# Cross-attention and a mixture-of-experts FFN on one core: softmax reciprocals spread through DRAM

## What is computed

```
xn    = layernorm(x)
q     = rmsnorm(xn Wq)           # 16 heads of 32
k, v  = rmsnorm(ctx Wk), ctx Wv  # per kind (text, image)
att   = softmax(q k_text / sqrt(32)) v_text + softmax(q k_img / sqrt(32)) v_img
x1    = x + att Wo
x2    = layernorm(x1)
out   = x1 + shared(x2) + sum over a token's 4 experts of weight * expert(x2)
```

## Time and profile before

| | |
|---|---|
| profiled execution, first to last instruction (span) | 1212.8 us |
| its own time | listed with the runs: 1212.84, 1211.41, 1212.59 us; the page gives the span only |
| TensorE, weight loads beside it | 1150.7 us busy (95%), 415.6 (34%) |
| VectorE | 824.9 us busy (68%) |
| ACT | 649.5 us busy (54%) |
| GpSimd | 190.7 us busy (16%) |
| granted TensorE clock, mean | 0.994 |
| DMA | 143.02 MB, mean 118 GB/s |

### The profile page before, as it was taken

The page is one execution under the profiler, slowest core; times in us unless marked ns, Lnnn a source line. Parts: engine busy times, 40 slices in busy tenths (PEclk is TensorE's granted clock), DMA queues, the critical chain, the costliest instruction groups (busy, mean ns, idle before and its releaser), DMA issues. The chain is left out here.

```text
span 1212.8 us, 20795 instructions
## 1 busy us (share of the span) xinstructions
PE 1150.7 (95%) x8484; PEld 415.6 (34%) x8484; DVE 824.9 (68%) x1042; ACT 649.5 (54%) x916; POOL 190.7 (16%) x299
## 2 busy tenths in 40 slices
PE   6899999999999999999999999998999998999996
PEld 2342222444222244422224442222454433333332
DVE  6776878877677887768788777997778852222221
ACT  5558997444899744499864459885121121222221
POOL 1220000143000014300001430001110012333342
PEclk9999999999999999999999999999899999999998
DMA  9851000559200045910004693013823317999742
GB/s 312 178 113 36 2 2 10 131 119 211 36 2 2 11 129 135 205 26 2 2 26 114 147 195 111 2 36 106 329 75 121 115 59 289 357 317 317 243 62 33
DMA packets 140056, 143.02 MB, mean 118 GB/s; under 512 B 107952, under 2 KB 108208, under 8 KB 134960
## 3 DMA queue, kind: packets, MB, share of 16 engines
q1 hardware_dynamic: 134832, 130.78, 36.9%
q0 software_dynamic: 5120, 10.82, 4.7%
HBM read 95.67 MB, written 20.73 MB: 96 GB/s over the span
## 5 line engine op out<-in xcount | busy, mean ns | idle before, releaser
L665 ACT ACTIVATE work<-ps 128x1024 f32<-128x1024 f32 (+1 forms) x416 | 403.0, 1021 | 42.5 <-PE ps L1152 38.8
L1158 PE MATMUL ps<-work,vals 128*32 128x512 f32 (+2 forms) x1664 | 221.0, 603 | 1.2 <-ACT work L665 0.6
L994 PE MATMUL ps<-wts,work 128*128 128x512 f16 x864 | 193.1, 379 | 2.7 <-DVE work L721 2.4
L1152 PE MATMUL ps<-quer,keys 32*128 32x512 f16 x2496 | 171.9, 378 | 16.0 <-ACT work L665 2.8
L900 DVE TENSOR_TENSOR work<-work 128x2048 f32<-128x2048 f32 x64 | 146.6, 2291 | 6.3 <-DVE work L897 0.5
L900 DVE TENSOR_TENSOR attn<-attn,work 128x2048 f32<-128x2048 f32 x62 | 142.0, 2290 | 5.2
L994 PEld LDWEIGHTS ps<-wts,work 128*128 128x128 f16 x864 | 83.8, 98 | 109.7 <-issue 8.3
L1961 PE MATMUL ps<-wring,xgt 128*80 128x512 f32 x256 | 114.9, 592 | 0.0
L586 ACT CAST work<-work 128x512 f16<-128x512 f32 x68 | 42.0, 618 | 130.8 <-DVE work L753 130.8
L994 PE MATMUL ps<-wts,hl 128*128 128x512 f16 x432 | 100.2, 383 | 11.6 <-DVE wts L703 7.5
L1152 PEld LDWEIGHTS ps<-quer,keys 32*128 32x128 f16 x2496 | 46.2, 92 | 185.1 <-ACT work L665 159.9
(11 more groups left out here) (216 smaller groups left out, 1364.7 us busy)
## 6 DMA issues: line engine op xcount, KB each, us to landing
wring<-in_wx SPq DMA_DIRECT2D x32, 1536.0 KB, 8.9
raw<-in_ctx SPq DMA_DIRECT2D x52, 256.0 KB, 3.1
work<-in_x SPq DMA_DIRECT2D x4, 1024.0 KB, 5.3
table<-nums SPq DMA_DIRECT2D x16, 256.0 KB, 2.5
work<-in_x SPq DMA_DIRECT2D x12, 256.0 KB, 5.1
x<-work SPq DMA_DIRECT2D x12, 256.0 KB, 2.6
x2t_rows<-nums SPq DMA_DIRECT2D x12, 256.0 KB, 2.5
x2t<-x2t_rows SPq DMA_DIRECT2D x3, 1024.0 KB, 9.2
```

Source lines behind the costliest of these rows:

```text
L665: act.activation(prob[0:rows, s % PROBS, 2 * half:2 * half + 2, :], ps[0:rows, 2 * pair:2 * pair + 2, :], ACT.Exp, scale=SCALE).then_inc(a ...
L994: mm = pe.matmul(out, lhs(a, c)[:, cols], wts[:, w, z, c * D:(c + 1) * D], start=(k == 0), stop=(k == len(steps) - 1))
L1152: mm = pe.matmul(ps[:, 2 * pair + h % 2, :], k[h * HD:(h + 1) * HD, :], q[h * HD:(h + 1) * HD, :], start=(e == 0), stop=(e == len(terms) - 1))
L1158: return pe.matmul(ps[h * HD:(h + 1) * HD, NUM, :], vals[a:z, ORDER[n], g * P + h * HD:g * P + (h + 1) * HD], prob[a:z, s % PROBS, h, :], ...
```

## The change

- `spread` on TensorE, the 0/1 tiles `sel`, and their banks go. SP stores `rcp` to a DRAM tensor (`store_sums`, in slot 1 of the next batch) and reads it back with the row repeated over 32 partitions: one DMA for each of the four heads h, for two head groups at a time, into a tile `rb`, in slots 1 and 5 (`spread_pair`). The second waits until the first two groups are weighed.
- `weigh(g)` multiplies by `rb` and runs two slots later (slots 3 to 6), with `out_high` and `out_low` behind it; `O_SLOT`, `NORM_SLOT` and `LOW_SLOT` move by two slots as well.
- For the last batch all eight DMAs (two sets of four) are issued ahead of the branch, into a tile `rbl` for all groups.
- Ahead of the branch TensorE computes gate half 0, up half 0 and gate half 1 (`gate`). Behind it `gate_up(1)`, without its gate half, `gate_up(2)` and `gate_up(3)` come before the output products. ACT and VectorE have the shared tiles' work reordered to match; the check matmul comes after the gates.
- Waits for earlier table and row stores move from ACT's to VectorE's list. Expert 2's load moves behind the last normalising. Some semaphores are merged for the second pass.

The core of the diff:

```diff
-O_SLOT = [6, 7, 10, 11]
+O_SLOT = [8, 9, 12, 13]
-NORM_SLOT = [8, 9, 12, 13]
-LOW_SLOT = [9, 10, 13, 14]
+NORM_SLOT = [10, 11, 14, 15]
+LOW_SLOT = [11, 12, 15, 16]
+WEIGH = 3
...
-        self.sel = at("sel", 172 * KB_, [P, NG, 2, P], F32)
+        self.rb = at("rb", 172 * KB_, [P, 2, 2, L], F32)
+        self.rbl = at("rbl", 164 * KB_, [P, NG, 2, L], F32)
...
+            def store_sums(bb):
+                sp.wait_ge(a_rcp, bb + 1)
+                sp.dma_start(r_dram[bb], rcp[:, :]).then_inc(s_rd, 16)
+
+            def spread(dst, bb, pair, landed):
+                for h in range(4):
+                    rows = r_dram[bb][h * HD + 4 * pair:h * HD + 4 * pair + 4, :]
+                    sp.dma_start(dst[h * HD:(h + 1) * HD].rearrange("p g t q -> p (g t) q"),
+                                 rows.unsqueeze(0).to_broadcast([HD, 4, L])).then_inc(landed, 16)
+
+            def spread_pair(bb, q, pair):
+                if pair == 0:
+                    sp.wait_ge(s_zero, 32)
+                    sp.wait_ge(s_rd, 16 * bb)
+                    upto(sp, a_at, q * NG)
+                else:
+                    sp.wait_ge(a_at, gn(q, 1))
+                spread(rb[:, :, :, :], bb - 1, pair, s_rb)
+
+            def last_spreads(bb):
+                store_sums(bb)
+                sp.wait_ge(s_rd, 16 * (bb + 1))
+                for pair in range(2):
+                    spread(rbl[:, 2 * pair:2 * pair + 2, :, :], bb, pair, s_rl[pair])
...
+                        if i == 1 and b > 0:
+                            store_sums(bb - 1)
                         if i >= 1:
                             turn_key(bb, i - 1)
+                        if i in (1, 5) and b > 0:
+                            spread_pair(bb, q, i // 4)
...
                 last_loads(p, bb)
+                last_spreads(bb)
...
             def weigh(q, g):
-                dve.wait_ge(a_sel, gn(q, g))
-                image = own(dve.tensor_tensor(nums[:, g, 1, :], nums[:, g, 1, :], ps[:, NUM, :], ALU.mult))
-                dve.tensor_tensor(nums[:, g, 0, :], nums[:, g, 0, :], ps[:, DEN, :], ALU.mult).then_inc(a_mt, 1)
+                dve.wait_ge(s_rb, 64 * (2 * q + g // 2 + 1))
+                image = own(dve.tensor_tensor(nums[:, g, 1, :], nums[:, g, 1, :], rb[:, g % 2, 1, :], ALU.mult))
+                dve.tensor_tensor(nums[:, g, 0, :], nums[:, g, 0, :], rb[:, g % 2, 0, :], ALU.mult).then_inc(a_mt, 1)
...
-                    if b > 0 and 1 <= i < 1 + NG:
-                        weigh(q, i - 1)
-                    if b > 0 and 2 <= i < 2 + NG:
-                        out_low(q, i - 2)
+                    if b > 0 and WEIGH <= i < WEIGH + NG:
+                        weigh(q, i - WEIGH)
+                    if b > 0 and WEIGH + 1 <= i < WEIGH + 1 + NG:
+                        out_low(q, i - WEIGH - 1)
...
-                    if b > 0 and 1 <= i < 1 + NG:
-                        spread(bb - 1, q, i - 1)
...
-                    steps = [(c, a, z) for c in range(NC) for a, z in PARTS]
-                    for k, (c, a, z) in enumerate(steps):
-                        pe.matmul(ps[:, GATE_BANK, :], swt[SG][:, a, c * D:c * D + P], m.x2t[0][:, :, z, c, :],
-                                  start=(k == 0), stop=(k == len(steps) - 1))
-                    pe.wait_ge(a_rcp, bb + 1)
-                    for t, bank in ((1, SEL_BANK[0][0]), (0, SEL_BANK[0][1])):
-                        pe.matmul(ps[:, bank, :], sel[:, 0, t, :], rcp[:, :], start=True, stop=True)
+                    gate(SG, 0, 0)
+                    pe.wait_ge(f_wlo, 3 * p + 2)
+                    gate(SU, 0, 2).then_inc(s_gate, 1)
+                    gate(SG, 1, 1)
...
+            gate(0)
             weigh(0)
+            gate_low(0)
             weigh(1)
+            gate(1)
             out_low(0)
             weigh(2)
             out_low(1)
+            gate_low(1)
             weigh(3)
             out_low(2)
...
             out_low(3)
-            gate(0)
-            gate_low(0)
-            gate(1)
+            gate(2)
+            gate_low(2)
             out_rows(0)
-            gate_low(1)
             out_norm(0)
             out_rows(1)
             norm_low(0)
             out_norm(1)
+            gate(3)
             out_rows(2)
...
-            for g in range(1, NG):
-                spread(g)
-            gate_up(0)
-            pe.wait_ge(t_mt, 2)
             gate_up(1)
+            gate_up(2)
+            gate_up(3)
             for j in range(QT):
                 output(j)
...
-            gate_up(2)
             turn_out(QT - 1)
             for j in range(3 * QT, NT):
                 rt_last = route(j)
             rt_last.then_inc(e_r, 1)
-            gate_up(3)
             gate_up(4)
```

More of the change, by code:

```diff
@@ L156, in __init__, with attention_program @@
         self.yf = [at(f"yf{i}", o * KB_, [CAP, D], F32) for i, o in enumerate((108, 110, 60, 62))]
-def attention_program(nc, m, d, x1_dram, x2_dram, table, out, s_turned, s_xr):
+def attention_program(nc, m, d, x1_dram, x2_dram, r_dram, table, out, s_turned, s_xr, s_rl, s_gate):
     with ExitStack() as ctx:
@@ L298, in value_bank, with turned, rowed @@
             return NUM if k == KT - 1 else 2 + k % 2
+        def turned(bb):
+            return (bb - B + 1) * (HEADS * QT + 1)
+        def rowed(bb):
+            return (bb - B + 1) * (2 + NG)
         def rows_of(n):
@@ L479, in _ @@
                 sp.wait_ge(s_turned[1], 64)
+                for pair in range(2):
+                    sp.wait_ge(s_rl[pair], 128)
             sp.end_ifs()
@@ L879, in sums_and_results @@
                         ffn_weight(p, g - 1)
+                    if b > 0 and g < 2:
+                        for j in range(2):
+                            dve.wait_ge((s_tab, s_x2)[g][j], 16 * ((out_batch(bb - 1) + 1) * QT // 2))
                     dve.wait_ge(a_img, gn(bb, g))
@@ L929, in maxima @@
                             bank = 4 * (k % 2)
-                            dve.wait_ge(m_sc, n0 + k + 1)
+                            dve.wait_ge(m_sc, turned(bb - 1) + k + 1)
                             flat = ps[:, bank:bank + 4, :].rearrange("p a n -> p (a n)")
@@ L982, in _ @@
                 one_pass(1)
+                for pair in range(2):
+                    dve.wait_ge(s_rl[pair], 128)
             dve.end_ifs()
@@ L1251, in attention, with gate @@
                     pe.wait_ge(f_wlo, 3 * p + 1)
-                    steps = [(c, a, z) for c in range(NC) for a, z in PARTS]
-                    for k, (c, a, z) in enumerate(steps):
-                        pe.matmul(ps[:, GATE_BANK, :], swt[SG][:, a, c * D:c * D + P], m.x2t[0][:, :, z, c, :],
-                                  start=(k == 0), stop=(k == len(steps) - 1))
-                    pe.wait_ge(a_rcp, bb + 1)
-                    for t, bank in ((1, SEL_BANK[0][0]), (0, SEL_BANK[0][1])):
-                        pe.matmul(ps[:, bank, :], sel[:, 0, t, :], rcp[:, :], start=True, stop=True)
+                    gate(SG, 0, 0)
+                    pe.wait_ge(f_wlo, 3 * p + 2)
+                    gate(SU, 0, 2).then_inc(s_gate, 1)
+                    gate(SG, 1, 1)
+            def gate(w, it, bank):
+                steps = [(c, a, z) for c in range(NC) for a, z in PARTS]
+                for k, (c, a, z) in enumerate(steps):
+                    mm = pe.matmul(ps[:, bank, :], swt[w][:, a, c * D + it * P:c * D + (it + 1) * P],
+                                   m.x2t[0][:, :, z, c, :], start=(k == 0), stop=(k == len(steps) - 1))
+                return mm
             def one_pass(p):
@@ L1300, in lay_attention, with ffn_program @@
     }
-def ffn_program(nc, m, d, x1_dram, table, out, s_turned):
+def ffn_program(nc, m, d, x1_dram, table, out, s_turned, s_rl, s_gate):
     with ExitStack() as ctx:
@@ L1491, in norm_store @@
                          ps[:, TURN_BANK[j], :].bitcast(F16)).then_inc(n_out, 1)
-            for g in range(NG):
-                out_high(g)
             gate_tanh(0)
             gate_high(0)
+            out_high(0)
             gate_tanh(1)
+            out_high(1)
             gate_high(1)
+            out_high(2)
+            out_high(3)
+            gate_tanh(2)
+            gate_high(2)
+            norm_high(0)
+            norm_high(1)
+            gate_tanh(3)
+            norm_high(2)
+            norm_high(3)
+            gate_high(3)
             for j in range(QT):
-                norm_high(j)
-            for j in range(QT - 1):
                 norm_store(j)
-            gate_tanh(2)
-            norm_store(QT - 1)
-            gate_high(2)
             act.wait_ge(e_r, 1)
@@ L1508, in _ @@
                            scale=-1.0 / WS).then_inc(e_ez, 1)
-            for n in range(3, 13):
+            for n in range(4, 13):
                 gate_tanh(n)
@@ L1675, in _ @@
             out_norm(3)
+            gate_low(3)
             norm_low(3)
-            gate(2)
             dve.wait_ge(s_const, N_CONST)
@@ L2016, in build @@
```

(6 more changed lines are left out.)

110 lines of the change are left out of this document (45 added, 65 removed).

## The result

The kernel after takes 1253.2 us (median of four runs, 1251.45 to 1254.95), the kernel before 1212.25 (1211.41 to 1212.84) on the same chip: a ratio of 1.0331 with a 95% interval of 1.0308 to 1.0354. It is slower by 41 us, where 10 were forecast and 1237 was the end of the range. The spans of the profiled executions are 1253.0 and 1212.8, so 40.2 us are to be found.

A forecast was written before the change was run, and what follows sets the result against it. TensorE, busy 95% of the span, was taken to bound the kernel, with VectorE close behind. The profiled 1212.8 us plus 7.5 for three stretches plus 2 for the hand-over gave 1222.3, taken as 1222; range 1205 to 1237.

The forecast's parts named there:

- Part 2: Three projection stretches: VectorE waits for the DMA round trip of the reciprocals; +2.5 us a batch, +7.5 for three.
- Part 3: Hand-over to the FFN: later check matmul, later block start and a longer norm chain; +2 us, bounds -3 to +6.
- T: First stretch: the time at which VectorE ends slot 4's `key_low`, put at 242.6.
- b): First stretch: context chunk 4, issued behind the store and first four DMAs, lands at 226.4; ACT's half done at 227.0.
- c): First stretch: VectorE then has 15.6 us of work to the end of slot 4's `key_low`, ending at 242.6.
- d): First stretch: VectorE's wait for the transpose and second four DMAs ahead of `weigh(2)`, taken as 6.4 us, bounds 5.0 to 10.
- the start of the FFN block: Hand-over: all engines start together, 5.9 us after the flag, the latest (SP) counting; 857 against 851.4 before.
- Part 1: TensorE loses four pairs of 0/1 products a batch: 7.2 us a batch, 21.6 for three, if VectorE and DMAs keep up.
- The rival of half rate: Projection stretches: DMAs to 32 partitions run at half rate, +6.3 us a batch more, total 1240; chance 0.17.
- Faster: Projection stretches: the round trip fits inside TensorE's lead, three stretches win 5 us; total 1205 with hand-over -3; chance 0.23.

The follow-up runs named there:

- run 10: Changed kernel with the old hand-over, chunk 4 ahead of the first DMA set, second set ahead of the transpose, groups 2 and 3 weighed a slot later: 1196.85 us.
- run 9: Changed kernel with the second DMA set issued ahead of the transpose and the first set behind the load of context chunk 4: 1221.46 us.
- run 3: Changed kernel with each spreading DMA carrying the same bytes to 128 partitions, from distinct rows of zeros: 1241.33 us.
- run 4: Changed kernel with each spreading DMA still to 32 partitions, but from distinct rows of zeros instead of a repeated row: 1253.42 us.
- run 1: Changed kernel with the second four DMAs issued ahead of the transpose of key slot 4: 1235.56 us.
- run 2: Changed kernel without the second four DMAs, groups 2 and 3 being weighed with the first two groups' factors: 1220.61 us.
- run 7: Changed kernel with all eight DMAs ahead of the branch, each cut to 16 columns, 8 KB in place of 256: 1246.58 us.
- run 5: Changed kernel's projections with the hand-over of the kernel before (0/1 products, gates where they stood): 1246.6 us.
- run 11: Changed kernel, its new hand-over kept, with chunk 4 first, second DMA set early, groups 2 and 3 weighed a slot later: 1203.93 us.
- run 6: Changed kernel without the store and the eight DMAs ahead of the branch, using leftover factors: 1248.74 us.
- run 12: Run 10's kernel with tile 0's up half ahead of the branch and gate-ups 1 and 2 ahead of the output products: 1197.43 us.

## Why the forecast was off

The direction was right, and every mechanism of Part 2 and Part 3 but one is in the trace. The sizes were not: a stretch cost 11.6 us where the sum had 2.5. Four steps failed. In Part 2, T in b) and c) (242.6, measured 246.4), the wait in d) (6.4, measured 9.2) and TensorE's clock, which the sum had at nothing (1.7 a stretch); in Part 3, the start of the FFN block.

- **Part 1** holds. With no long gap a stretch gains 4.8 us of the 7.2 (run 10). In the first stretch 1.5 of the rest are gaps that grew: 1.42, 0.62 and 1.71 in run 10 against 0.88, 0.63 and 0.75 before.
- **Step b**, +3.4 us. The store of the reciprocals was awaited 1.5 us longer than forecast, so chunk 4 was issued at 222.78 (224.3 by the old clock, 1.0 late), and ACT's half starts at 228.29, 5.5 after the issue, not 3.1: the chunk stands behind the first four, with the DMA engines 95% busy at 217 GB/s from 221 to 228.5. T came at 246.4 by the old clock, not at 242.6 (c) adds the other 0.4). In the kernel after, the delay reaches slot 7 by way of T; TensorE's own gap ahead of chunk 4's key, 3.6 us, is covered there by the longer one ahead of slot 7. With the second set early it shows: run 9 took out the delay and won 12.3 us in three stretches.
- **Step d**, +2.8 us: the wait is 9.2 (8.7 on average over the three), within the bounds (5.0 to 10) and not the 6.4 taken. The working let SP's issues limit it, of transfers that run alone; the DMA engines do, which are full during the wait. Part of it is the rate to 32 partitions: run 3 takes 0.9 off the average wait. The other 1.4 above the forecast stay in run 3; the small packets of the transposes around the set are the likely cause, which no run takes away by itself.
- **The rival of half rate**, given 0.17, had the rate about right (223 against 387 GB/s, 0.58), and its "against" (two of four DMAs go to the other half) does not hold: four DMAs in order to the four quarters of the partitions still come at that rate. Its terms, +2.9 for the wait and +3.4 for T, are near the measured +2.8 and +3.8, but partly by luck, since run 3 puts only 0.9 of the wait down to it. They sum to 1241, and not to its 1240; what it lacks to 1253 is the clock and the attention's start (8.1 us in three stretches) and more at the hand-over. The Trainium skill (SBUF — State Buffer, "Door 1: The DMA port swizzle") gives the two rates from which the prediction had estimated a wait of 8.7. Runs 3 and 4 agree with it that the destination's partitions set the rate; that the average wait is 8.7 as well is luck in the same way.
- **Not in the sum**: the clock. Behind a gap of 3.6 or 10 us the next product starts at the lower clock and takes 4.1 to 5.3 us in place of 2.75, +1.7 in this stretch; ahead of slot 7 that adds to the stretch, at chunk 4 the longer gap covers it. Also the start of attention, +1.0 a batch (a wait for ACT of 1.7 in place of 0.75), which I put down to normalising ending two slots later, without a run on it. With steps b and d these make 3.8 + 2.8 + 1.7 + 1.0 = 9.3 of the 9.1 that a stretch cost above the forecast of 2.5; that sum is arithmetic on the first stretch, and only its larger parts were taken away by themselves (runs 1, 2 and 9).
- **Part 3**: the check matmul is late by the 2.8 forecast (5.55 became 8.50 after the reciprocal); the outputs start 15.7 us after the block as forecast. The failed step is the start of the block: "All engines start the FFN block together", and "the latest one counts". SP came 1.4 us after the flag, and that would have been nearly free (run 7). What counted were the 2 MB in flight: with them the block begins 6.5 us later than in run 7, which has the same DMAs without the bytes. That it is the fetch of the block's own instructions that is held up is read from the packets of queues 8 and 14. So the hand-over cost +9.3 up to the outputs, -4.3 behind them; run 5 puts the whole at 6.6, against +2 forecast and a bound of +6. The forecast start, 857, was 5.6 us late; the block came 12.3 - 6.0 + 2.9 = 9.3 late.
- **Where the working chose badly.** The wait stood on VectorE's queue, which has little slack, and each choice in b) and d) took the price of a transfer running alone. Both were next to other transfers.
- **Faster** was not impossible: runs 10 and 11 show that the round trip fits inside TensorE's lead, once both sets are issued ahead of what SP waits for and the second has a slot more. Its condition was T plus the wait below 246.5; here it is 246.4 + 9.2 = 255.6.

The Trainium skill (Runtime: NRT & Kernel Launch, "Instruction fetch mechanics") says that a taken branch to a page that isn't loaded forces a DMA fetch before the engine can go on. The instruction queues' packets between flag and block agree; that the block waits while data is in flight is what runs 6 and 7 add.

Left open: why the experts take 3.1 us more (the same part varies by 4 us between these kernels); whether the fetch waits by place in the DMA engines' queues or by their share (in run 4 four instruction packets moved at 884.7 to 885.7, in the middle of the data, and the block still came 10.1 us after the flag); and what makes the rest of the wait in run 3, whose packets are also smaller, 2 KB in place of 8.

## What to carry to other kernels

A DMA that takes over a matmul's job is priced by the wait on the engine that consumes it, and by what stands ahead of it in the issuing queue: the same 24 DMAs cost 34 us here or win 15 (runs 5 and 10), by which side of one transpose and one chunk load they are issued on, and one slot of slack. Price a transfer beside its neighbours, and one to 32 partitions lower than one to 128 (223 against 387 GB/s here). Keep large transfers away from a branch to another program: here 2 MB in flight held the next block up by 6.5 us.

## What the runs showed of the hardware

- 256 KB to 32 partitions land in a median of 4.5 us, 3.7 when spread over 128; in flow, eight such DMAs move 223 GB/s against 387 to 128 (run 3), with the DMA engines full at the lower rate too. Repeated or distinct source rows made no difference (1253.2 and 1253.4 us).
- From flag to block it takes 5.3 to 5.9 us with little data in flight, and 10.1 to 12.3 with 2 MB to 32 partitions a DMA in flight (7.9 when they go to 128, 8.3 for the DRAM copies, which may have another cause).
- At the end of a gap of 10 us TensorE is granted 0.50; a product of twelve then takes 4.4 us in place of 2.75 (5.3 in the third stretch). After gaps of 3.6 to 5.1 us the same product took 4.1 to 5.3. Below that it went both ways: 2.75 after a gap of 2.78 (run 1), but 4.44 after one of 2.73 (run 3), and 7.04 in place of 5.35 for 24 matmuls after one of 2.77 (run 12).
